# Attention: direction 1's largest sender score per receiver taken from the stored count matrix, ahead of direction 0

## The reference

```python
def _attention_aggregate(h_proj, sender, receiver, attn_vec, num_nodes):
    h_sender = h_proj[sender]
    h_receiver = h_proj[receiver]
    e = jnp.einsum('ehd,hd->eh', h_sender, attn_vec[:, :HD]) + jnp.einsum('ehd,hd->eh', h_receiver, attn_vec[:, HD:])
    e = jax.nn.leaky_relu(e, NEG_SLOPE)
    e_max = jax.ops.segment_max(e, receiver, num_segments=num_nodes)
    alpha = jnp.exp(e - e_max[receiver])
    alpha_sum = jax.ops.segment_sum(alpha, receiver, num_segments=num_nodes)
    alpha = alpha / (alpha_sum[receiver] + EPS_SOFTMAX)
    msg = h_sender * alpha[..., None]
    return jax.ops.segment_sum(msg, receiver, num_segments=num_nodes)
...
h_in = _attention_aggregate(h_proj, src, dst, a_in, n)
h_out = _attention_aggregate(h_proj, dst, src, a_out, n)
```

## Time and profile before

| | |
|---|---|
| median of 3 runs | 3301.39 us (3297.81 to 3304.03) |
| the profiled execution's own time | 3297.36 us |
| span of the profiled execution | 3295.5 us |
| PE busy | 2192.3 us (67%) |
| DVE busy | 2205.0 us (67%) |
| POOL busy | 1638.3 us (50%) |
| ACT busy | 847.4 us (26%) |
| mean granted TensorE clock | 0.828 of full speed |

### The profile page before, as it was taken

The page is one execution under the profiler, slowest core; times in us unless marked ns, Lnnn a source line. Parts: engine busy times, 40 slices in busy tenths (PEclk is TensorE's granted clock), DMA queues, the critical chain, the costliest instruction groups (busy, mean ns, idle before and its releaser), DMA issues.

```text
span 3295.5 us, 47742 instructions
## 1 busy us (share of the span) xinstructions
PE 2192.3 (67%) x12658; PEld 1222.6 (37%) x12659; DVE 2205.0 (67%) x3520; ACT 847.4 (26%) x1397; POOL 1638.3 (50%) x1455
## 2 busy tenths in 40 slices
PE   0488888887959799994962444444566666638563
PEld 0233343333434355543551111111466511118563
DVE  8999888887468600255043444445987799989777
ACT  0099533331001300022000111111344322206342
POOL 7400133332077777777005777777877777710000
PEclk9899999999989899997975565555559999955897
DMA  2000011112435344301905434435358733530453
GB/s 72 0 0 0 25 50 50 50 50 73 154 83 171 81 96 101 56 1 22 192 20 110 112 112 116 115 112 102 93 164 270 237 112 111 100 33 0 141 178 91
DMA packets 195115, 301.52 MB, mean 91 GB/s; under 512 B 120540, under 2 KB 133818, under 8 KB 194922
## 3 DMA queue, kind: packets, MB, share of 16 engines
q1 hardware_dynamic: 138986, 175.88, 17.0%
q0 software_dynamic: 40512, 62.87, 10.6%
q10 hardware_dynamic: 15552, 61.94, 6.0%
HBM read 191.65 MB, written 88.01 MB: 85 GB/s over the span
## 4 chain that ended last, share of the span: by engine, by line
PE 38%; POOL 20%; issue 17%; DVE 14%; DMA 5%; ACT 5%; ACTq 1%; DVEq 0%; SPq 0%; POOLq 0%; PEldq 0%
POOL arena L1294 19%; PE PS L536 13%; PE PS L680 9%; PE PS L865 6%; DMA arena<-T_att,idx 4%; ACT arena L512 4%; PE PS L962 3%; PE PS L474 2%; PE PS L949 1%; DVE arena L1185 1%; DVE arena L372 1%; DVE arena L558 1%; DVE arena L488 1%; PE PS L1231 1%; DVE arena L557 1%
## 5 line engine op out<-in xcount | busy, mean ns | idle before, releaser
L1294 POOL DMA_INDIRECT arena<-T_att,idx x864 | 844.9, 978 | 314.0 <-issue 228.8
L536 PE MATMUL PS<-arena 128*128 128x400 f16 (+2 forms) x4320 | 760.9, 321 | 238.9 <-issue 131.1
L1129 DVE TENSOR_REDUCE arena<-PS 128x1024 f32 (+1 forms) x432 | 506.6, 1249 | 317.0 <-PE PS L1096 317.0
L536 PEld LDWEIGHTS PS<-arena 128*128 128x128 f16 (+2 forms) x4320 | 452.2, 137 | 538.0 <-issue 346.9
L1467 POOL DMA_INDIRECT order<-arena x400 | 505.6, 1264 | 249.5 <-issue 249.5
L1096 PE MATMUL PS<-arena,pick 128*128 128x512 bf16 x864 | 335.1, 493 | 140.7 <-DVE arena L1129 136.3
L680 PE MATMUL PS<-arena 128*128 128x512 f16 (+1 forms) x1575 | 318.0, 361 | 88.3 <-issue 75.2
L557 DVE TENSOR_SCALAR arena<-arena 128x512 f16<-128x512 f16 x448 | 275.7, 615 | 62.6 <-PE PS L536 61.6
L1085 PE MATMUL PS<-ident_b,score_buf 128*32 128x128 bf16 x864 | 90.0, 267 | 301.4 <-ACT score_buf L1058 292.1
L614 POOL TENSOR_TENSOR rdeg<-rdeg,arena 128x1600 f32<-128x1600 f32 x48 | 154.3, 3216 | 265.1 <-ACT arena L598 265.1
L680 PEld LDWEIGHTS PS<-arena 128*128 128x128 bf16 x1575 | 147.8, 99 | 254.6 <-issue 103.1
(11 more groups left out here) (259 smaller groups left out, 2914.8 us busy)
## 6 DMA issues: line engine op xcount, KB each, us to landing
spill<-arena SPq DMA_DIRECT2D x108, 560.0 KB, 2.9
arena<-spill ACTq DMA_DIRECT2D x108, 560.0 KB, 3.7
arena<-A SPq DMA_DIRECT2D x50, 800.0 KB, 4.5
A<-arena SPq DMA_DIRECT2D x50, 400.0 KB, 2.4
arena<-A SPq DMA_DIRECT2D x50, 400.0 KB, 3.2
arena<-T_att,idx POOLq DMA_INDIRECT x864
order<-arena POOLq DMA_INDIRECT x400
T_att<-h SPq DMA_DIRECT2D x2, 1600.0 KB, 13.3
```

What stands on the lines that cost most here:

```text
L536: return t.matmul(where, lhsT, rhs, start=False, stop=True, skip_group_check=True)
L1129: v.tensor_reduce(cmax[d][:, u:u + 2, bass.ds(i * SLOTS + half * GROUP + q // 2 * QUAD, QUAD)], PS[:, u * BANK:(u + 2) * BANK].rearrange(" ...
L1294: p.indirect_dma_start(out=ring1[:, b, j, :], out_offset=None, in_=T_att[d][:, :], in_offset=bass.IndirectOffsetOnAxis(ap=idx[:, d, k:k + ...
```

## The change

Direction 1 no longer goes through `top`. Its maxima come from A: for a tile of 128 receivers (rows of A) and a band of 1600 senders (columns), ACT makes a mask in PSUM that is 0 where an edge exists and 2^100 where not, and one DVE instruction per head subtracts the mask from the senders' scores, spread over all partitions, and keeps the largest. That is 25 tiles x 2 bands x 4 heads = 200 such instructions. This runs before `top(0)`. Its parts:

- Ahead of it, four small DVE multiplications make `send_w`; PE multiplies it with `hT` into the senders' score rows of 3200 columns for 4 heads (`brow_pe`), and DVE and ACT copy these out of PSUM, 1536 and 1664 columns each.
- `dense_act` loads the 25 strips of A (800 KB each) from ACT's queue into three buffers and makes 50 masks of 128x1600, in two halves of PSUM by turns.
- `dense_dve` is the loop of 200; then one maximum over the two bands, four PE transposes, and the receiver's score and the leaky ReLU on 25 rows, which gives `mT`.
- In `guard(1)`, scans and fold are gone. PE spreads the receivers' scores and then `mT` over the chunks, and DVE copies each out.
- In both directions the addition of the senders' score parts moves from the front of guard to behind the look-up loop, and there waits for `scores_here` of the whole direction.
- The digits of direction 1 are gone. POOL's stream, the spills and `weighted` are as before.

```diff
+        def brow_pe(t):
+            t.wait_ge(wx_ready, 2)
+            for hd in range(HEADS):
+                for c, cut in enumerate(BROW_CUT):
+                    if hd:
+                        t.wait_ge(brow_read[c], hd)
+                    for a0 in range(cut.start, cut.stop, BANK):
+                        a1 = min(a0 + BANK, cut.stop)
+                        last = t.matmul(PS[:, a0:a1], send_w[:, hd, :], hT[:, a0:a1], start=True, stop=True)
+                    last.then_inc(brow_summed, 1)
...
+        def dense_act(a):
...
+            for k in range(TILES):
+                a.wait_ge(strip_here[k % RING], 16 * ((3 * TILES + k) // RING + 1))
+                for b in range(BANDS):
+                    n = BANDS * k + b
+                    if n >= BANDS:
+                        a.wait_ge(dense_used, HEADS * (n - BANDS + 1))
+                    band = slice(b * BW, (b + 1) * BW)
+                    a.activation(mask_slot(b), dense_strip[k % RING][:, band], ACT.Relu,
+                                 bias=big_col[:, 0:1], scale=NEG_BIG).then_inc(mask_ready, 1)
+                if k + RING < TILES:
+                    a.wait_ge(mask_ready, BANDS * (k + 1))
+                    dense_fetch(a, k + RING)
...
+        def dense_dve(v):
...
+                    for hd in range(HEADS):
+                        n = (BANDS * k + b) * HEADS + hd
+                        if n >= 2:
+                            v.wait_ge(dense_used, n - 1)
+                        v.tensor_tensor_reduce(dense_junk[n % 2], score_row[:, hd, band], mask_slot(b), 1.0, NEG_BIG,
+                                               ALU.subtract, ALU.max, dense_max[:, b, hd, k:k + 1]) \
+                            .then_inc(dense_used, 1)
...
+            if d == 0:
+                chunk_max_dve(v, d)
...
+            else:
+                v.wait_ge(recv_summed, 2)
+                v.tensor_copy(mr[d][:, HEADS:, :], recv).then_inc(recv_read, 1)
+                v.wait_ge(recv_summed, 3)
+                v.wait_ge(recv_read, 1)
+                dve_link(v.tensor_copy(mr[d][:, 0:HEADS, :], recv))
...
             v.wait_ge(er_ready, 2 + GB[d] + GR[d])
+            v.wait_ge(scores_here, GB[d] + GR[d])
+            dve_link(v.tensor_tensor(sender[d], sE[d][:, :, 0:HEADS].rearrange("p k h -> p h k"),
+                                     sE[d][:, :, HEADS:2 * HEADS].rearrange("p k h -> p h k"), ALU.add))
+            dve_link(v.tensor_tensor(sender[d], sender[d], sE[d][:, :, 2 * HEADS:].rearrange("p k h -> p h k"), ALU.add))
...
+            dense_dve(v)
             dve_link(v.tensor_copy(steps_at, iota[:, 0:P]))
             v.sem_inc(scaled_ready, 1)
             v.sem_inc(reduced, 2)
             v.sem_inc(er_ready, 2)
+            top_dve(v, 0)
+            v.wait_ge(round_done, 1)
             for d in range(2):
-                top_dve(v, d)
-                v.wait_ge(round_done, d + 1)
                 guard_dve(v, d)
                 weighted_dve(v, d)
                 weighted_out_dve(v, d)
```

More of the change, by code:

```diff
@@ L243, in gnn_kernel @@
               for a, e in ((h[:, :, :].rearrange("p t f -> p (t f)"), EDGE[0]), (W, EDGE[1]))]
-        low = [W[:, at:at + c].bitcast(BF16).rearrange("p (k n) -> p k n", n=2) for at, c in ((2688, CH[0]), (3104, CH[1]))]
-        high = [W[:, at:at + c // 2].bitcast(BF16) for at, c in ((3552, CH[0]), (3760, CH[1]))]
+        low = W[:, 2688:2688 + CH[0]].bitcast(BF16).rearrange("p (k n) -> p k n", n=2)
+        high = W[:, 3104:3104 + CH[0] // 2].bitcast(BF16)
         digit_i = view(18816, 4 * CHUNKS).bitcast(I32).rearrange("p (n k) -> p n k", n=4)
@@ L248, in gnn_kernel @@
         eq = OH_flat.bitcast(BF16).rearrange("p (g j e) -> p g j e", g=LAP, j=GROUP)
+        score_row = view(0, HEADS * NP_).rearrange("p (h n) -> p h n", h=HEADS)
+        dense_strip = [view(at, NP_ // 2).bitcast(F16) for at in (16128, 12800, 14400)]
+        dense_junk = [view(at, BW // 2).bitcast(BF16) for at in (17728, 21568)]
+        send_w = view(21056, HEADS * P).rearrange("p (h m) -> p h m", h=HEADS)
+        dense_max = W[:, 3990:3990 + 2 * HEADS * TILES].rearrange("p (b h t) -> p b h t", b=2, h=HEADS)
+        mT = view(28512, HEADS * P, TILES).rearrange("p (h e) -> p h e", h=HEADS)
+        BROW_CUT = (slice(0, 3 * BANK), slice(3 * BANK, NP_))
         steps_at = PS[:, 7 * BANK:7 * BANK + P]
@@ L316, in gnn_kernel @@
         rT_summed, rT_ready = sem("rT_summed"), sem("rT_ready")
+        brow_summed, brow_read = sem("brow_summed"), [sem(f"brow_read{c}") for c in range(2)]
+        mask_ready, dense_used = sem("mask_ready"), sem("dense_used")
+        recv_read = sem("recv_read")
         sT_summed, sT_ready = sem("sT_summed"), sem("sT_ready")
         masked_ready, reduced = sem("masked_ready"), sem("reduced")
-        recv_summed, mr_ready, mrb_ready = sem("recv_summed"), sem("mr_ready"), sem("mrb_ready")
+        recv_summed, mrb_ready = sem("recv_summed"), sem("mrb_ready")
         scores_here, scores_brought = sem("scores_here"), sem("scores_brought")
@@ new lines, in dense_fetch, with mask_slot @@
+        def dense_fetch(a, k):
+            a.dma_start(dense_strip[k % RING], A[k * P:(k + 1) * P, :]).then_inc(strip_here[k % RING], 16)
+        def mask_slot(b):
+            return PS[:, b * BQ * BANK:b * BQ * BANK + BW]
+        def dense_act(a):
+            dense_fetch(a, 0)
+            for hd in range(HEADS):
+                a.wait_ge(brow_summed, 2 * hd + 2)
+                a.copy(score_row[:, hd, BROW_CUT[1]], PS[:, BROW_CUT[1]]).then_inc(brow_read[1], 1)
+            for k in range(1, RING):
+                dense_fetch(a, k)
+            a.wait_ge(brow_read[0], HEADS)
+            a.wait_ge(brow_read[1], HEADS)
+            for k in range(TILES):
[10 more added lines that the diff above has]
+                    dense_fetch(a, k + RING)
@@ new lines, in gnn_kernel @@
+        DENSE = BANDS * TILES * HEADS
+        def dense_dve(v):
+            for hd in range(HEADS):
+                v.wait_ge(brow_summed, 2 * hd + 1)
+                v.tensor_copy(score_row[:, hd, BROW_CUT[0]], PS[:, BROW_CUT[0]]).then_inc(brow_read[0], 1)
+            for c in range(2):
+                v.wait_ge(brow_read[c], HEADS)
+            for k in range(TILES):
+                for b in range(BANDS):
+                    v.wait_ge(mask_ready, BANDS * k + b + 1)
+                    band = slice(b * BW, (b + 1) * BW)
+                    for hd in range(HEADS):
+                        n = (BANDS * k + b) * HEADS + hd
[4 more added lines that the diff above has]
+                            .then_inc(dense_used, 1)
+            v.wait_ge(dense_used, DENSE)
+            v.tensor_tensor(dense_max[:, 0, :, :], dense_max[:, 0, :, :], dense_max[:, 1, :, :], ALU.max) \
+                .then_inc(dense_used, 1)
+            v.wait_ge(rT_summed, 2)
+            turned_max = PS[0:TILES, 0:HEADS * P].rearrange("p (h e) -> p h e", h=HEADS)
+            dve_link(v.tensor_tensor(mT, turned_max, rT[:, 1, :, :], ALU.add))
+            v.scalar_tensor_tensor(mT, mT, 0.2, mT, ALU.mult, ALU.max).then_inc(rT_ready, 1)
@@ L1049, in gnn_kernel, with tile_max_pe @@
+        def tile_max_pe(t):
+            t.wait_ge(dense_used, DENSE + 1)
+            for hd in range(HEADS):
+                last = t.transpose(PS[0:TILES, hd * P:(hd + 1) * P], dense_max[:, 0, hd, :], ident)
+            last.then_inc(rT_summed, 1)
+            t.wait_ge(rT_ready, 2)
         QUAD = 4
@@ L1215, in guard_pe @@
         def guard_pe(t, d):
[L1216 removed]
+            if d == 0:
+                t.wait_ge(reduced, 2 + UNITS * GR[0])
             for hd in range(HEADS):
@@ L1220, in guard_pe @@
             last.then_inc(recv_summed, 1)
+            if d:
+                t.wait_ge(recv_read, 1)
+                for hd in range(HEADS):
+                    last = t.matmul(PS[:, hd * BANK:hd * BANK + CH[d]], mT[:, hd, :], tile_sel[:, d, 0:CH[d]],
+                                    start=True, stop=True)
+                last.then_inc(recv_summed, 1)
             t.wait_ge(mrb_ready, d + 1)
@@ L1454, in _ @@
             p.memset(zeros[:, :], 0.0)
+            p.memset(big_col[:, :], -NEG_BIG)
             p.memset(eps[:, :], 1e-5).then_inc(zeros_ready, 1)
@@ L1541, in _ @@
             norm_dve(v, 3, True)
+            v.wait_ge(wx_ready, 1)
+            for hd in range(HEADS):
+                last = v.tensor_scalar(send_w[:, hd, :], ones, Wx[:, 8 + hd:9 + hd], None, ALU.mult)
+            last.then_inc(wx_ready, 1)
             v.wait_ge(hT_ready, HT_DONE + 1)
@@ L1571, in _ @@
             v.tensor_copy(figures, iota[:, 0:BASE])
[L1572 to L1580, removed]
+            whole = digit_i[:, 0, 0:CH[0]]
+            parts_i = digit_i[:, 1:, 0:CH[0]]
+            dve_link(v.tensor_scalar(whole, key[:, 0, 0:CH[0]], 1.0, None, ALU.add))
+            v.tensor_scalar(parts_i[:, 0, :], whole, BASE - 1, None, ALU.bitwise_and)
```

(9 more changed lines are left out.)

24 lines of the change are left out of this document (11 added, 13 removed).

## The result

The changed kernel took 3191.63 us (median of four runs, 3185.07 to 3199.40) against 3300.59 us for the kernel before beside it: a ratio of 0.967, 95% interval 0.9646 to 0.9695. The forecast was 3184, with 3160 to 3240 as range. Its profiled execution took 3185.07 us with a span of 3183.3.

A forecast was written before the change was run, and what follows sets the result against it. POOL's gather stream was taken to bound the kernel: its end at 2930, plus 6.7 for additions and 241.0 behind, gave a 3178 span, 3180 as profiled execution, and with 4.0 for the median 3184 us; range 3160 to 3240.

The forecast's parts named there:

- The stream bounds top(0), and its end bounds guard(1)'s successor: POOL's gathers pace top(0) before the change; after it, DVE waits in guard(1) for the last cast, about 50 us to spare.
- Score rows on PE: PE's f32 products for four heads' score rows, ahead of the dense instructions: 30 to 46 us, taken as 38.
- Dense steps: The 200 mask-and-maximum steps on DVE: 1.80 to 2.03 us each, taken as 1.90, 380 us, ending at 2168.
- Top(0) at 4.83 us a group: Top(0) on DVE, now with a backlog of gathered groups: 52 groups at 4.83 us, 251 us, ending at 2427.
- Guard(0) and weighted(0): Direction 0's stages on DVE after top(0): 327.7 us as before, ending at 2755.
- Guard(1) before its splits: PE spreads twice (3 to 6 us each) and DVE copies twice (2.0 each): about 14 us, ending at 2769.
- DVE's slack: DVE reaches its wait for the last group's scores at 2877, before the stream finishes: about 50 us to spare.
- The stream, +19 us forecast: POOL's gathers end at 2930 instead of 2910.8: start +1, strips +8 (0 to 20), guard(1)'s splits +10 (5 to 20).
- the 2950 that was named as a sign of being wrong: The forecast would be wrong if the stream's last cast came after 2950; it was expected near 2930.
- The tail, 6.7 + 241.0 us: After the stream: 6.7 us for the two score-part additions, then 241.0 from the exponential's argument to the span's end.
- The rival of locked-out gathers: Only one gather passes per dense step: 200 in 380 us instead of 301, stream 127 us late, median 3311; 8%.
- The rival of the slow pair: Dense instruction plus column write exceeds 2.17 us: 3250 at 2.5, a loss above 2.75, about 3430 at half rate; 11%.

The follow-up runs named there:

- second profile of the changed kernel: The changed kernel run once more, unedited, beside the kernel before: 3185.86 us, ratio 0.9663; its profiled execution took 3193.95 us.

## Why the prediction was right

The side, the size (117 us forecast, 112 in span, 109 in medians) and the mechanism came out. Step by step:

- **The stream bounds top(0), and its end bounds guard(1)'s successor.** Right, by the 104.9 us of idle time released by the cast, and by the two runs with added steps: the first 76 us free, and beyond the slack nearly one for one.
- **Score rows on PE, 38 us taken, 30 as lower end.** Mis-sized. PE worked on them from 1742.8 for 24.2 us, below the lower end, with the granted clock at 0.87 over 1740 to 1770. A head's 3200 columns take 5.4 us, at a granted clock of 1.00 (1753.5 to 1758.9), as DVE's copies of two heads show:

```profile
1748.11 1.76 DVE L1108 COPY arena<-PS 128x1536 f32<-128x1536 f32 x1 [5.38 <-PE PS L1070]
...
1753.48 1.76 DVE L1108 COPY arena<-PS 128x1536 f32<-128x1536 f32 x1 [3.62 <-PE PS L1070]
```

  The lower end was no full-clock price: during the 7.48 us of the earlier trace rows the granted clock was 0.56 up to 1730 and 0.96 after it, 0.77 on average, which makes 5.8 us at full clock if the product goes with the clock (an estimate), and the other row, 5.91 us at 0.50 for 1664 columns, makes 5.7 for 3200 in the same way. PE also began 3 us ahead of the forecast's 1745.8. First dense step at 1770.4 instead of 1788.
- **Dense steps, 1.90 us taken of 1.80 to 2.03.** Mis-sized, as 1.742 lies below the lower bound too. The step is 1.742 us: the main instruction takes 1.815, as the f32 pair of the earlier trace rows (1.820), but overlaps its neighbour by 0.07, and the accumulator's read of 0.08 us runs beside the next main instruction. I had bounded from below by 1.80 because I scaled four reductions of 1024 columns with their fixed part; 200 steps took 348 us, not 380. Nothing hung on it, as this is inside the slack.
- **Top(0) at 4.83 us a group.** Right: 250.5 us from 2126.2 to 2376.7 against 251.
- **Guard(0) and weighted(0).** 329.8 us against 327.7.
- **Guard(1) before its splits.** 17 us instead of 14: each spread by PE took 6.5 us, just above the upper end of 3 to 6, at half clock (0.50).
- **DVE's slack.** Forecast 53 us, measured 104.9; the two mis-sized terms make up 50 of the difference of 52; guard(1)'s 3 us more and the stream's 5 us more nearly cancel.
- **The stream, +19 us forecast.** +24.6. The strips cost 13 us by counting gathers and about 10 by leaving them out (8 taken), the splits 7 to 11 (10 taken), and the start was 1 us earlier, not later. These bounds held. In the second profile of the changed kernel the last cast came at 2944.0, 33 us later than before, near the 2950 that was named as a sign of being wrong; why the stream's end moves so between executions was not settled.
- **The tail, 6.7 + 241.0 us.** 6.7 + 241.1.
- **The rival of locked-out gathers.** It did not occur, and the reason given, the operand in PSUM, was shown by putting it in SBUF: +86 us. That the price was 86 for half the steps says that all of them in SBUF would have cost more than the whole gain, if it scales (an estimate, not run). The rival had taken one gather per step; with 75 long gathers to 100 such steps it was priced too low.
- **The rival of the slow pair.** It did not occur. The Trainium skill, "Vector Engine (DVE) Microarchitecture Reference", section "Points that are easy to get wrong", has the scalar-tensor-tensor form with two SBUF sources that are not bf16 at half throughput: no run here shows half rate, not even with two f32 sources in SBUF and an accumulator (1.81 us for 1600 columns). The instruction here is a custom one, so the rule may still hold for the form that it names with an accumulator. The prediction's 3.41 us for a half-rate step comes without its working; twice the 1.82 us of the earlier trace rows would be 3.64.
- **What I had not seen** is that "leaves out top(1)" and "moves the additions" are each nearly worthless: 0.3% and 0.0% by themselves. The forecast priced them together without saying so.

## What to carry to other kernels

When a stream on one queue sets the pace, ask of each later stage which of its instructions really needs the stream's last element, and let the wait stand there and no earlier: here one wait in its old place cost 101 us, nine tenths of the gain, and cutting the next stage in two blocks gained another 89. Work that needs nothing from the stream belongs where the engines wait for it, and its cost is then its disturbance of the stream: measure it by counting the stream's steps per window. Extra dummy work is a cheap test of slack; if 76 us more change nothing, that engine does not decide.

## What the runs showed of the hardware

- **The accumulator's read hides.** Two instructions per step, 1.815 and 0.08 us, pass in 1.742 us from start to start, with a wait for the step before last in each and no idle time recorded. Where each step waits for the one just before it, as in the 40 added ones, it is 1.86 us.
- **Both operands in SBUF hold up indirect gathers.** This holds for the custom instruction too: gathers of 1.4 to 2.4 us against 0.94, and 65 fewer in 347 us. The Trainium skill, "SBUF — State Buffer", section "Who interferes with whom", says that an instruction with at most one SBUF input outside the two-port modes does not contend with GpSimd; the steps with the mask in PSUM agree (0.94 us beside them).
- **The granted clock in one stage at two paces.** PE did nothing for the 347 us of the dense stretch, at a granted clock of 0.50, and then ran top(0) at the high level; before, in the same stage paced by the gathers, it stood at 0.54, but top(1), paced by DVE and without such a rest before it, ran at 0.95. Windows of the changed kernel (width, busy and count of PE, PEld, DVE, ACT, POOL, clock, DMA share, GB/s):

```profile
2120.00:2380.00 260.00, 154.31 (x817) 49.15 (x840) 256.06 (x322) 61.11 (x104) 198.06 (x224) 0.99 0.43 110
2380.00:2500.00 120.00, 74.33 (x833) 67.49 (x832) 112.08 (x123) 53.91 (x53) 96.33 (x91) 0.50 0.33 99
```

  In the first window the clock stands at the upper of its two levels (2.4 GHz), in the second, guard(0), at the lower (1.2 GHz), and in both PE had been at work for about six tenths of the time. What made it rise and fall again was not tested. Nor was what it is worth here: top(0) is DVE's at 4.82 us a group, and no run has a DVE-paced top at the lower clock.
